# Second attention: own queries and keys projected for two batches at a time, in every second step

## The reference, cut to what matters

```
qkv   = x  @ Wqkv     + bqkv          # own queries, keys, values
qkv_a = xa @ Wqkv_aux + bqkv_aux      # keys and values of the context
main  = softmax(q k^T / 4)  v         # 100 x 100 per head
aux   = softmax(q ka^T / 4) va        # 100 x 361 per head
out   = ((1 - gate) * main + gate * aux) @ Wo + bo
```

## Time and profile before

| | |
|---|---|
| median of 3 runs | 1222.9 (1222.24 to 1226.67) |
| profiled execution | 1222.04, span 1220.3 |
| PE busy | 1164.6 (95%) |
| DVE, ACT, POOL busy | 596.4 (49%), 478.2 (39%), 390.7 (32%) |
| mean granted TensorE clock | 0.987 |

### The profile page before, as it was taken

The page is one execution under the profiler, slowest core; times in us unless marked ns, Lnnn a source line. Parts: engine busy times, 40 slices in busy tenths (PEclk is TensorE's granted clock), DMA queues, the critical chain, the costliest instruction groups (busy, mean ns, idle before and its releaser), DMA issues. The chain is left out here.

```text
span 1220.3 us, 29213 instructions
## 1 busy us (share of the span) xinstructions
PE 1164.6 (95%) x11433; PEld 899.5 (74%) x11433; DVE 596.4 (49%) x1437; ACT 478.2 (39%) x1130; POOL 390.7 (32%) x411
## 2 busy tenths in 40 slices
PE   6999999977999999998999999999998999999998
PEld 4767777755999999975566666666665589999975
DVE  5777777775211101047867667567656511122126
ACT  3545555522332333224544454454454133322221
POOL 3666766642222222131001011011021245555510
PEclk9999999977999999999999999999999999999999
DMA  6001011405999998732021001000000469999964
GB/s 186 22 27 38 26 36 34 136 8 183 386 335 319 329 333 321 278 104 55 2 87 33 14 20 33 14 9 9 2 15 17 164 213 357 356 350 351 343 221 163
DMA packets 64392, 180.93 MB, mean 148 GB/s; under 512 B 10176, under 2 KB 36608, under 8 KB 55808
## 3 DMA queue, kind: packets, MB, share of 16 engines
q1 hardware_dynamic: 55088, 156.40, 37.5%
q0 software_dynamic: 8064, 22.03, 5.0%
q10 hardware_dynamic: 1104, 0.64, 0.2%
HBM read 163.11 MB, written 15.93 MB: 147 GB/s over the span
## 5 line engine op out<-in xcount | busy, mean ns | idle before, releaser
L2344 ACT ACTIVATE ex_hT<-kept_psum,ex_w 128x128 f32<-128x128 f32 x464 | 132.2, 368 | 295.0 <-PE kept_psum L2399 169.7
L2399 PE MATMUL kept_psum<-ex_xT,ex_w 128*128 128x128 f32 x1856 | 222.5, 276 | 0.0
L2399 PEld LDWEIGHTS kept_psum<-ex_xT,ex_w 128*128 128x128 f32 x1856 | 215.6, 193 | 0.1
L2410 PE MATMUL kept_psum<-ex_w,ex_hT 128*128 128x256 f32 x928 | 213.9, 379 | 0.0
L2306 DVE TENSOR_TENSOR ex_yt<-kept_psum,ex_b 128x256 f32<-128x256 f32 x84 | 35.7, 425 | 352.9 <-PE kept_psum L2410 352.9
L2410 PEld LDWEIGHTS kept_psum<-ex_w,ex_hT 128*128 128x128 f32 x928 | 170.1, 190 | 19.7
L2272 POOL DMA_INDIRECT ex_results<-ex_yt,ex_to_row x84 | 82.8, 986 | 254.7 <-DVE ex_yt L2306 254.7
L1273 ACT ACTIVATE at_probs<-kept_psum 120x800 f32<-120x800 f32 (+2 forms) x128 | 101.1, 841 | 77.0 <-PE kept_psum L1455 77.0
L1097 DVE TENSOR_REDUCE at_negmax<-kept_psum 100x2 f32<-100x722 f32 x128 | 115.4, 902 | 0.0
L568 ACT ACTIVATE at_probs<-kept_psum 120x800 f32<-120x800 f32 (+1 forms) x96 | 80.0, 836 | 73.6 <-PE kept_psum L691 73.5
L410 DVE TENSOR_REDUCE at_negmax<-kept_psum 120x8 bf16<-120x800 f32 (+1 forms) x96 | 90.6, 985 | 23.7 <-PE kept_psum L682 23.3
(11 more groups left out here) (256 smaller groups left out, 1688.6 us busy)
## 6 DMA issues: line engine op xcount, KB each, us to landing
ex_w<-in_pack_in SPq DMA_DIRECT2D x32, 1028.0 KB
ex_w<-in_pack_out SPq DMA_DIRECT2D x32, 1024.0 KB
ex_w<-in_pack_in SPq DMA_DIRECT2D x52, 514.0 KB
ex_w<-in_pack_out SPq DMA_DIRECT2D x52, 512.0 KB
at_ctx<-in_ctxT SPq DMA_DIRECT2D x31, 361.0 KB, 3.7
ex_normed<-ex_xhat SPq DMA_DIRECT2D x16, 200.0 KB
ex_w<-ex_results SPq DMA_DIRECT2D x6, 400.0 KB
ex_sw<-in_L_ffn_sW SPq DMA_DIRECT2D x2, 1024.0 KB
```

Of the source, the lines that this page charges most:

```text
L2344: last = act.activation(hT[t % N][:, c, :], ps_h[:, (t * U + u) % N, i * P:(i + 1) * P], ACT.Gelu, bias=w1[t % N][:, B1 + c:B1 + c + 1])
L2399: last = pe.matmul(ps_h[:, (t * U + u) % N, i * P:(i + 1) * P], w1[t % N][:, c * ff + f:c * ff + f + P], xT[t % N][:, c, :], start=(c == 0 ...
L2410: last = pe.matmul(ps_y[:, t % N, 0:D], hT[t % N][:, c, :], w2[t % N][:, c * D:(c + 1) * D], start=(c == 0), stop=(c == FC - 1))
```

## The change

`x_pair(t)` takes the place of `x_batch(t)`: in even steps t = 0 ... 12 the batches 2p and 2p + 1, p = t / 2 + 1, are transposed one after the other and projected together, in odd steps none. Queries and keys are projected apart (`project_pair`), each into a ring bank of its own (own_q, own_k), with 200 columns a matmul; queries before `by_key(t, 2)` and keys behind it (in step 12 both later). ACT takes them by `take_own_q` and `take_own_k`. Tiles xT and qz become one tile each with 4 places instead of 3. The sums of aux are now also halved in the odd steps (`halved`). In steps 13 and 14 `turn_sums(t - 2, 1)` moves behind `by_key(t, 2)`, with two `keep_warm` matmuls after it. `moments(1)` is made ahead of the loop, and the rows of batches 2 and 3 are normalized at the start of step 0. The diff's core:

```diff
-    NC, NK, NX, NQ, NV, PRE = early.NC, early.NK, 3, 3, 3, 2
+    NC, NK, NX, NQ, NV, PRE = early.NC, early.NK, 4, 4, 3, 2
-    def x_batch(t):
-        return t + 2 if 0 <= t < B - 2 else None
+    def x_pair(t):
+        return t // 2 + 1 if t % 2 == 0 and 0 <= t < B - 3 else None
...
-    ORDER = (("max", 0), ("key0", NK - 1), ("key1", NK - 1), ("sum_main", -1), ("turn_main", -2), ("xT", 2), ("sum_aux", -1),
-             ("turn_aux", -2), ("own", 2), ("value01", 1), ("mixT", -2), ("value2", 1), ("out", -2),
-             ("value_own", 0))
+    ORDER = (("max", 0), ("key0", 4), ("key1", 4), ("sum_main", -1), ("turn_main", -2), ("xT", 2), ("xT", 3), ("sum_aux", -1),
+             ("turn_aux", -2), ("own_q", 2), ("own_k", 2), ("value01", 1), ("mixT", -2), ("value2", 1), ("out", -2), ("value_own", 0))
+    LIGHT_ORDER = (("max", 0), ("value01", 1), ("value2", 1), ("sum_main", -1), ("turn_main", -2), ("xT", 2), ("xT", 3), ("sum_aux", -1),
+                   ("turn_aux", -2), ("own_q", 2), ("mixT", -2), ("value_own", 0), ("own_k", 2), ("out", -2))
...
+    def halved(t):
+        return spread_out(t) or t % 2 == 1 and on(t)
...
# vector: ahead of the loop, and in step 0 behind maxima(1, 0)
+        moments(1)
...
             if t == 0:
-                moments(1)
+                newton(1)
+                normed(2)
+                normed(3)
...
# scalar
+        def take_own_q(p):
+            act.wait_ge(ready["own_q"], p)
+            need(act, by_key_ready, (2 * p + 2 - NQ) * UNITS)
+            bank, slot = ring_bank("own_q", p), 2 * p % NQ
+            for i in range(KC):
+                by_batch = bank[:, i * 2 * T:(i + 1) * 2 * T].rearrange("p (b t) -> p b t", t=T)
+                for a in range(2):
+                    last = act.activation(qz[:, slot:slot + 2, i, a, :], by_batch, ACT.Identity, bias=bqm[:, i, a:a + 1], scale=own[:, a:a + 1])
+            last.then_inc(taken["own_q"], 1)
+
+        def take_own_k(p):
+            act.wait_ge(ready["own_k"], p)
+            need(act, by_key_ready, (2 * p + 2 - NK) * UNITS)
+            bank = ring_bank("own_k", p)
+            for i in range(KC):
+                for j in range(2):
+                    at = (2 * i + j) * T
+                    last = act.activation(kT[(2 * p + j) % NK][:, i, 0:T], bank[:, at:at + T], ACT.Identity, bias=bqk[:, KC + i:KC + i + 1])
+            last.then_inc(taken["own_k"], 1)
...
             if on(t):
                 exponents(t, 1)
-            if x_batch(t) is not None:
-                take_xT(x_batch(t))
+            if x_pair(t) is not None:
+                take_xT(2 * x_pair(t))
+                take_xT(2 * x_pair(t) + 1)
             if on(t - 1):
                 take_sum(t - 1, 1)
-            if x_batch(t) is not None and not spread_out(t):
-                take_own(x_batch(t))
+            if x_pair(t) is not None and not spread_out(t):
+                take_own_q(x_pair(t))
...
             if on(t):
                 exponents(t, 2)
-            if x_batch(t) is not None and spread_out(t):
-                take_own(x_batch(t))
+            if x_pair(t) is not None:
+                if spread_out(t):
+                    take_own_q(x_pair(t))
+                else:
+                    take_own_k(x_pair(t))
...
# tensor
+        def project_pair(name, p):
+            bank, slot = into(name, p), 2 * p % NX
+            pe.wait_ge(taken["xT"], 2 * p + 2)
+            for i in range(KC):
+                at = ((KC if name == "own_k" else 0) + i) * P
+                for c in range(KC):
+                    last = pe.matmul(bank[:, i * 2 * T:(i + 1) * 2 * T], w[:, c, at:at + P], xT[:, slot:slot + 2, c, :],
+                                     start=(c == 0), stop=(c == KC - 1))
+            last.then_inc(ready[name], 1)
...
             if on(t):
                 by_key(t, 1)
-            if x_batch(t) is not None:
-                turn_x(x_batch(t))
+            if x_pair(t) is not None:
+                turn_x(2 * x_pair(t))
+                turn_x(2 * x_pair(t) + 1)
             if on(t - 1):
-                sum_up(t - 1, 1, range(HG // 2 if spread_out(t) else HG))
+                sum_up(t - 1, 1, range(HG // 2 if halved(t) else HG))
             if t == 0:
-                keep_warm(into("own", 2), 3)
+                keep_warm(into("own_q", 1), 3)
             if on(t + 1):
                 by_query(t + 1, 2)
-            if spread_out(t):
+            if halved(t):
                 sum_up(t - 1, 1, range(HG // 2, HG))
-            if on(t - 2):
+            if on(t - 2) and t not in (B - 3, B - 2):
                 turn_sums(t - 2, 1)
...
-            if x_batch(t) is not None and not spread_out(t):
-                project_own(x_batch(t))
+            if x_pair(t) is not None and not spread_out(t):
+                project_pair("own_q", x_pair(t))
             if on(t):
                 by_key(t, 2)
-            if x_batch(t) is not None and spread_out(t):
-                project_own(x_batch(t))
+            if x_pair(t) is not None:
+                project_pair("own_q" if spread_out(t) else "own_k", x_pair(t))
+            if t in (B - 3, B - 2):
+                turn_sums(t - 2, 1)
+                keep_warm(into("mixT", t - 2), 2)
...
             if spread_out(t):
                 values_own(t)
+                if x_pair(t) is not None:
+                    project_pair("own_k", x_pair(t))
```

More of the change, by code:

```diff
@@ L938, in attend1 @@
     xhat = [m.sb(f"xhat{i}", [T, D]) for i in range(2)]
-    xT = [m.sb(f"xT{i}", [P, KC, T]) for i in range(NX)]
-    qz = [m.sb(f"qz{i}", [P, KC, 2, T]) for i in range(NQ)]
+    xT, qz = m.sb("xT", [P, NX, KC, T]), m.sb("qz", [P, NQ, KC, 2, T])
     shift = m.sb("shift", [P, HS, T], BF16)
@@ L951, in attend1 @@
     rden_ready, mixed_ready, mix_ready = m.sem("rden_ready"), m.sem("mixed_ready"), m.sem("mix_ready")
-    ORDER = (("max", 0), ("key0", NK - 1), ("key1", NK - 1), ("sum_main", -1), ("turn_main", -2), ("xT", 2), ("sum_aux", -1),
-             ("turn_aux", -2), ("own", 2), ("value01", 1), ("mixT", -2), ("value2", 1), ("out", -2),
-             ("value_own", 0))
-    LIGHT_ORDER = (("max", 0), ("value01", 1), ("value2", 1), ("sum_main", -1), ("turn_main", -2), ("xT", 2), ("sum_aux", -1),
-                   ("turn_aux", -2), ("own", 2), ("mixT", -2), ("value_own", 0), ("out", -2))
+    ORDER = (("max", 0), ("key0", 4), ("key1", 4), ("sum_main", -1), ("turn_main", -2), ("xT", 2), ("xT", 3), ("sum_aux", -1),
+             ("turn_aux", -2), ("own_q", 2), ("own_k", 2), ("value01", 1), ("mixT", -2), ("value2", 1), ("out", -2), ("value_own", 0))
+    LIGHT_ORDER = (("max", 0), ("value01", 1), ("value2", 1), ("sum_main", -1), ("turn_main", -2), ("xT", 2), ("xT", 3), ("sum_aux", -1),
+                   ("turn_aux", -2), ("own_q", 2), ("mixT", -2), ("value_own", 0), ("own_k", 2), ("out", -2))
     NO_VALUES_ORDER = (("max", 0), ("key0", 4), ("key1", 4)) + LIGHT_ORDER[3:]
@@ L965, in spread_out @@
         return t in LIGHT or t in NO_VALUES
+    def halved(t):
+        return spread_out(t) or t % 2 == 1 and on(t)
     first_own_taken = m.sem("first_own_taken")
-    ready = {n: m.sem(f"{n}_ready") for n, _ in ORDER}
-    taken = {n: m.sem(f"{n}_taken") for n, _ in ORDER}
-    ready["own_more"], taken["own_more"] = m.sem("own_more_ready"), m.sem("own_more_taken")
+    NAMES = list(dict.fromkeys(n for n, _ in ORDER)) + ["own", "own_more"]
+    FIRST = {"key0": KEYED, "key1": KEYED, "own_q": 1, "own_k": 1}
+    ready = {n: m.sem(f"{n}_ready") for n in NAMES}
+    taken = {n: m.sem(f"{n}_taken") for n in NAMES}
     x_ready = taken["out"]
@@ L974, in used @@
     def used(n, off, t):
-        b = key_batch(t) if n in ("key0", "key1") else x_batch(t) if n in ("xT", "own") else t + off
+        if n in ("xT", "own_q", "own_k"):
+            p = x_pair(t)
+            return None if p is None else 2 * p + off - 2 if n == "xT" else p
+        b = key_batch(t) if n in ("key0", "key1") else t + off
         return b if b is not None and on(b) and not (n in ("value01", "value2") and b <= PRE) else None
@@ L1181, in vector @@
                 maxima(t + 1, 1)
-            if t == 0:
-                newton(1)
-                normed(2)
             if on(t - 2):
@@ L1200, in vector @@
                 normalize(t - 2, 1)
-            if t == 0:
-                normed(3)
             if t == 1:
@@ L1239, in take_xT @@
             need(act, ready["value_own"], b - NX + 1)
-            act.activation(xT[b % NX][:, :, :], ring_bank("xT", b)[:, 0:KC * T].rearrange("p (c t) -> p c t", c=KC),
+            act.activation(xT[:, b % NX, :, :], ring_bank("xT", b)[:, 0:KC * T].rearrange("p (c t) -> p c t", c=KC),
                            ACT.Copy).then_inc(taken["xT"], 1)
+        def take_own_q(p):
[16 more added lines that the diff above has]
+            last.then_inc(taken["own_k"], 1)
         def take_own(b):
@@ L1245, in take_own @@
             act.wait_ge(masks_set, 4)
```

(26 more changed lines are left out.)

## The result

The changed kernel took 1226.5 us (median of 16; 1225.1 to 1228.8) against 1223.0 before: ratio 1.0026, interval 1.0019 to 1.0034. By the ratio it is slower by 3.2 us (the medians differ by 3.5), within the band of 0.5%; the forecast was +2.2 us, a time of 1225. The profiled execution took 1225.13, 3.1 above that of before. (One run of the kernel before, 1943 us, is left out of the ratio.)

The account below looks back on a forecast made before the run. PE's instruction stream was taken to bound the second attention. Terms +12.8 - 9.95 + 2.35 - 2.15 - 0.35 - 0.5 sum to +2.2 us, forecast 1225 us; its own range 1222 to 1227, 8 in 10 for 1217 to 1230.

Parts of the forecast that it names:

- PE bounds the stage: Second attention: PE's instruction stream sets the time, busy 334.5 of 347 us, so only less PE work can gain.
- Projection: Projections of batches 2 to 15: a pair takes 3.0 us instead of 3.7, 5 us less PE work over 7 pairs.
- Bank wait: Even steps 2 to 12: sums of aux wait for ACT to take the first xT, 1.37 us each, 8.2 in all.
- Nothing behind it: Even steps: no later wait could swallow the delay of the sums, and ACT's eviction of own_q stays hidden.
- Odd steps: Steps 3 to 11 (odd) lose projection and transpose, halved sums cost 0.2 more: -1.95 us each, five times -9.75.
- Step 3: Third step of the second attention: besides the odd-step saving, a wait on DVE goes, 0.2 us more; -2.15 in all.
- Step 14: Late step of the second attention: turned sums and warming fill the 1.02 us PE waited for exponentials, -0.35 us.
- Steps 0, 1, 12 and 13: First and late steps of the second attention: 0 and 1 together -0.5 us, 12 +2.35, 13 -2.15.
- Rival 3: Even steps: granted clock falls as PE stands over 1 us; about 10 us, with the rest +12, 1235 us; chance 0.03.

## Why the prediction was right, and where it was off

- **PE bounds the stage.** Right: step lengths follow PE's stream; less PE work (4.0 us) and more waiting add up to the span.
- **Projection.** Forecast 187 ns a record of 200 columns, an estimate on a line between two rows; measured 181 (1.45 us for 8). Each projection is 0.05 shorter than forecast, 0.7 us in all.
- **Bank wait.** Forecast 1.37 us in six steps, the second transpose inside it. Measured: in step 2 the sums start 1.95 after the first transpose (605.69 to 607.64) against 0.57 before, which is 1.38. Of this PE stands idle for 1.00 (0.95 from step 6 on), and the rest is the second transpose. It was shown as the cause twice, by ACT's order and by the ring's.
- **Nothing behind it.** Right: 1.04 us a step came back when the wait went. ACT's four activations of own_q took 1.75 where 1.7 was estimated, and PE never waited for them in steps 2 to 10.
- **Odd steps.** -1.80 instead of -1.95. The halves cover a wait of 0.82 (0.9 forecast).
- **Step 3** got shorter by 0.6 more than forecast. Before, it had an idle time of 0.52 that no engine explains, and it is gone; that the change took it away is not shown, since one such of 1.41 came up in the experiment with 100 columns.
- **Step 14** is the term of the prediction that failed. "Turned sums and warming fill the 1.02 us": they do, but the order of DVE was not followed past the mix, and a wait of 1.28 for maxima takes the place of the one filled. Forecast -0.35, measured +0.80. The other steps together came out 1.0 below their forecasts, mostly by the smaller projection and the idle time of step 3. That these nearly cancel in the sum, +2.4 against +2.2, is luck.
- **Steps 0, 1, 12 and 13** came out within 0.2 of their forecasts. No experiment took their terms apart (`moments(1)` ahead of the loop, the warming, the moved sums of step 13), so the single terms are not shown.
- **Clock.** Rival 3 put the fall into every even step and had 0.03. It does not happen there: the clock is 1.00 behind every wait of 1.0 us. But it happens in step 0, in two of six profiles, at 1.5 us each, behind the 1.4 us wait for xT, which the prediction had in its account of step 0 as time only. The same instructions and the same wait left it at 1.00 in the other four; what decides was not seen. As a mean the fall would be 0.5 us, perhaps a part of why the ratios make the changed kernel 3.2 and 4.5 us slower where the profiled pair says 3.1; that the unprofiled runs have it was not seen. The rule weighed there says that micro-idling between groups of matmuls at bank changes makes the clock fall and rise (the Trainium skill, "TensorE: Matmul & The Clock Gate", section "A second HAM failure mode: psum-queue depth-cycling"). In steps 2 to 12 the traces do not bear it out, with 1.00 throughout; the two falls to 0.51 in step 0, each behind a single longer wait, are as near as they come to it.

## What to carry to other kernels

When an operation is added to a ring of few buffers, write the ring's list out and look at the new neighbour two places back of each use: a cheap transpose came to stand there, and its release sat on another engine behind 1.6 us of work. What repaired it was the order on the engine that releases, or the ring's order. A moved instruction is to be followed through the whole queue of the next engine, not only to its first consumer.

## What was not expected of the hardware

- The granted clock fell to 0.51, the level of 1.2 GHz, after PE had stood idle 1.4 us in step 0, among shorter waits and warming matmuls. This was so in 2 of 6 profiles of the same order of work. It did not fall behind waits of 1.0 us in full steps.
- A matmul of 200 columns as two pieces of 100, 200 apart, cost 181 ns a record: no more than the prediction's estimate from its rows of 128 and 256 columns (185). The same width in one piece was not run.
- ACT took 1.75 us for four activations of 200 columns and 1.41 for four of 100, so 100 columns more cost about 0.08 us each.
